# Expert tiles whose gathered rows are turned by VectorE after twelve moves per tile, and weights fetched by ScalarE's queue into two buffers

## What is computed

```python
x = x + tanh(g_xattn[0]) * ssm(ctx_1024, layernorm(x), ...)      # a selective scan (Mamba), 16 states, 512 channels
h = layernorm(x)
scores = softmax(h @ gate_w.T); the 6 best of 16 experts, weights normalised
out = sum over the chosen experts e of c[t, e] * swiglu_e(h[t])   # 512 -> 352 gate and up, 352 -> 512 down
out = out + swiglu_shared(h)                                     # 704 wide, done as two experts of 352
x = x + tanh(g_ffn[0]) * out
```

## Time and profile before

| | |
|---|---|
| median of 3 runs | 1429.51 us (1429.09 to 1432.42) |
| profiled execution, its own time | 1428.72 us |
| its span, first to last instruction | 1426.5 us |
| TensorE busy, instructions | 1342.8 us (94%), 8480 |
| VectorE, ScalarE, GpSimd busy | 785.2 (55%), 730.5 (51%), 948.6 (66%) us |
| granted TensorE clock, mean | 0.979 |
| routed tiles in the profile | from 692.97 to about 1408 us |

### The profile page before, as it was taken

One profiled execution on the slowest core, in us unless ns is written; L12 is line 12 of the kernel. 1 busy time (PEld: TensorE's weight loads), 2 busy tenths in 40 slices (PEclk: granted clock), 3 DMA queues, 4 the chain that ended last, 5 costly groups with the idle time before them and its releaser, 6 DMA issues.

```text
span 1426.5 us, 31834 instructions
## 1 busy us (share of the span) xinstructions
PE 1342.8 (94%) x8480; PEld 1208.7 (85%) x8481; DVE 785.2 (55%) x1364; ACT 730.5 (51%) x1317; POOL 948.6 (66%) x671
## 2 busy tenths in 40 slices
PE   6898998998898899999999999999999999999996
PEld 2676787887888799999999999999999998999995
DVE  6889898898999854653333333333333333333331
ACT  5899897898889464343332333323333333333321
POOL 0589899998998757887456665566645666646632
PEclk8899999998999999999999999999999999999998
DMA  4121123122241454645455535555445544455432
GB/s 138 38 75 31 54 68 102 66 93 69 76 160 68 135 123 103 146 81 141 84 144 143 132 62 146 140 144 142 105 94 139 143 134 101 102 146 133 76 67 36
DMA packets 65042, 149.13 MB, mean 105 GB/s; under 512 B 16976, under 2 KB 17616, under 8 KB 62656
## 3 DMA queue, kind: packets, MB, share of 16 engines
q0 software_dynamic: 31024, 62.10, 22.8%
q1 hardware_dynamic: 33392, 81.21, 17.3%
q10 hardware_dynamic: 560, 4.98, 0.9%
HBM read 101.50 MB, written 48.99 MB: 105 GB/s over the span
## 4 chain that ended last, share of the span: by engine, by line
PE 63%; DVE 3%; issue 2%; DVEq 1%; ACT 1%; POOL 1%; ACTq 0%; POOLq 0%
PE bank L1719 19%; PE bank L1699 18%; PE bank L1700 17%; PE bank L1687 3%; PE bank L1710 3%; DVE hs L1172 1%; PE bank L1604 1%; PE bank L1590 1%; PE bank L1602 1%; DVEq L1375 0%; POOL hc L949 0%; ACT ah L862 0%; DVE sc L1226 0%; PE bank L1665 0%; DVEq L1369 0%
## 5 line engine op out<-in xcount | busy, mean ns | idle before, releaser
L949 POOL TENSOR_TENSOR hc<-hs,crow 128x512 f32<-128x512 f32 x254 | 322.4, 1305 | 87.3 <-DVE hs L1172 81.5
L1699 PE MATMUL bank<-w,xh 128*128 (+1 forms) x1088 | 366.3, 338 | 6.2 <-DVE am L1393 2.9
L1700 PE MATMUL bank<-w,xh 128*128 (+1 forms) x1088 | 351.1, 323 | 0.0
L1015 POOL DMA_INDIRECT out_x<-ys,aid x104 | 169.8, 1633 | 271.3 <-issue 213.6
L1172 DVE TENSOR_TENSOR_SCAN hs<-dA,bank 128x512 f32<-128x512 f32 x256 | 295.6, 1208 | 46.2 <-PE bank L1604 28.8
L1719 PE MATMUL bank<-w,ah 128*128 (+1 forms) x816 | 264.8, 405 | 2.7 <-DVE al L1399 2.7
L1399 DVE TENSOR_TENSOR al<-bank,ah 128x384 fp32r<-128x384 f32 x136 | 75.9, 558 | 330.9 <-ACT ah L862 326.1
L1699 PEld LDWEIGHTS bank<-w,xh 128*128 128x128 f32 x1088 | 204.4, 188 | 26.0 <-issue 21.0
L1700 PEld LDWEIGHTS bank<-w,xh 128*128 128x128 f32 x1088 | 206.4, 190 | 4.1
L868 ACT COPY ys<-bank 128x512 f32<-128x512 f32 x136 | 79.8, 587 | 200.5 <-PE bank L1719 200.5
L1700 PE MATMUL bank<-w,xl 128*128 (+1 forms) x544 | 175.9, 323 | 0.0
(11 more groups left out here) (184 smaller groups left out, 2064.2 us busy)
## 6 DMA issues: line engine op xcount, KB each, us to landing
wraw<-in_wall SPq DMA_DIRECT2D x16, 2176.0 KB
crow<-c_rows SPq DMA_DIRECT2D x64, 256.0 KB, 3.3
xt<-token_rows_turned SPq DMA_DIRECT2D x32, 256.0 KB, 3.2
out_x<-ys POOLq DMA_DIRECT2D x32, 256.0 KB, 4.2
wraw<-in_wall ACTq DMA_DIRECT2D x2, 2176.0 KB
token_rows<-rowb SPq DMA_DIRECT2D x4, 1028.0 KB, 6.1
xrow<-in_x SPq DMA_DIRECT2D x4, 1024.0 KB, 7.5
out_x<-xrow SPq DMA_DIRECT2D x4, 1024.0 KB, 4.9
```

The source lines that it names most:

```text
L949: nc.gpsimd.tensor_tensor(hc[:, j, :], hs[:, j, :], crow[:, n % 4, :], ALU.mult).then_inc(hc_done, 1)
L1015: pool.indirect_dma_start(out_rows, bass.IndirectOffsetOnAxis(ap=aid[:, s:s + 1], axis=0), ys[:, s, :], None, bounds_check=TOKENS - 1, oob ...
L1699: nc.tensor.matmul(gate_bank[:, 0:I], xx, columns(w, off + ww + k * 2 * I, I), start=first, stop=last)
L1700: mm = nc.tensor.matmul(up_bank[:, 0:I], xx, columns(w, off + ww + k * 2 * I + I, I), start=first, stop=last)
```

## The change

1. `norm_chunk` writes the normalised rows with their features permuted: block (b, a) of 32 features goes to place (a, b). Weight rows of shared sets 0 and 1 and of the gate are loaded in that order (`fetch_turned`, five DMAs a set, four for the gate).
2. `turn_x` is removed. In its place, per routed tile: SyncE issues 12 DMAs (`move`), each of a block of 32 partitions x 128 columns from `xt` to `xs`, so that quarter g of the partitions goes to column block g; ScalarE copies the four blocks that stay on their own partitions (`keep`, ahead of `a_high`); VectorE transposes 32x32 blocks of `xs` into `xq` (`turn`, ahead of `a_low`). `x_high` and `x_low` read `xq` in place of the PSUM bank. `gather` waits for the moves and the copies of the tile that had its buffer.
3. SyncE's fetches of weights go. ScalarE issues the fetch of set e+1 behind its `split_high(e)`, into one of two buffers (`raws`, at offsets 0 and `FAR`).
4. GpSimd reads the table once per tile: row 3 of `meta` now holds the number of the set at its first tile, and 0 elsewhere.

```diff
+Q = 32
+G = P // Q
+MOVES = G * (G - 1)
+FAR = 33280
-               8: [("exp", 3)], TT - 3: [("fetch", 2)]}
+               8: [("exp", 3)], TT - 3: [("fetch", 2)], TT + 5: [("fetch", 3)]}
+        raws = alloc(span, "raws", [P, FAR + WCOLS])
+        xs = alloc(ctx, "xs", [P, 4, TC * P])
+        xq = alloc(ctx, "xq", [P, 2, H])
...
+        def quarters_in(eng, t, s, m, who):
+            apart(eng, moved[s], 16 * MOVES * ((t - NS) // 4 + 1) if isinstance(t, int) else 16 * MOVES * (m + 1), who)
+            apart(eng, kept, t + 1, who)
+        def fetch_turned(eng, e):
+            for b in range(G):
+                eng.dma_start(wraw[b * Q:(b + 1) * Q, 0:W2AT].rearrange("c (a i) -> c a i", a=G),
+                              wall[e, :, b * 2 * I:(b + 1) * 2 * I].rearrange("(a c) i -> c a i", c=Q)).then_inc(raw_in, 16)
+            eng.dma_start(wraw[:, W2AT:WCOLS], wall[e, :, W2AT:WCOLS]).then_inc(raw_in, 16)
...
 @block.sync
-            def fetch(e):
-                at_least(sp, wl_done, e)
-                sp.dma_start(wraw[:], wall[bass.ds(e, 1)].rearrange("a p c -> p (a c)")).then_inc(raw_in, 16)
+            def move(t, s, m):
+                rows_in(sp, t, s, m, "sp")
+                apart(sp, xt_turned, t - 3, "sp")
+                for a in range(G):
+                    for g in range(G):
+                        if g != a:
+                            sp.dma_start(xs[a * Q:(a + 1) * Q, s, g * P:(g + 1) * P],
+                                         xt[g * Q:(g + 1) * Q, s, a * P:(a + 1) * P]).then_inc(moved[s], 16)
-            with sp.Fori(3, NX) as e:
-                fetch(e)
             sp.wait_ge(meta_ready, 2)
+            groups = routed_groups(sp)
+            with sp.Fori(0, groups) as i:
+                for k in range(4):
+                    move(4 * i + NS + k, k, i)
...
 @block.scalar
-                nc.scalar.activation(rowb[:, t, 0:H], xrow[:, b % 2, t, :], ACT.Identity, ...
+                nc.scalar.activation(rowb[:, t, 0:H].rearrange("p (a b c) -> p b a c", a=G, c=Q),
+                                     xrow[:, b % 2, t, :].rearrange("p (b a c) -> p b a c", a=G, c=Q), ACT.Identity, ...
@@ split_high
-                nc.scalar.copy(columns(w, (e % 2) * 2 * WCOLS, mine), wraw[:, 0:mine]).then_inc(wh_done, 1)
+                nc.scalar.copy(columns(w, (e % 2) * 2 * WCOLS, mine), raws[:, bass.ds((e % 2) * FAR, mine)]).then_inc(wh_done, 1)
+                apart(act, wl_done, e, "act")
+                act.dma_start(raws[:, raw_at(e + 1)], wall[bass.ds((e + 1) % NX, 1)].rearrange("a p c -> p (a c)")).then_inc(raw_in, 16)
@@ x_high
-                    source = banks[4][:]
+                    source = xq[:, s, :]
+            def keep(t, s, m=None):
+                rows_in(act, t, s, m, "act")
+                act.wait_ge(xt_turned, t - 3)
+                for a in range(G):
+                    own = nc.scalar.copy(xs[a * Q:(a + 1) * Q, s, a * P:(a + 1) * P], xt[a * Q:(a + 1) * Q, s, a * P:(a + 1) * P])
+                own.then_inc(kept, 1)
@@ the loop
                     t, s = 4 * i + PEELED + k, (3 + k) % 2
+                    keep(t + 1, k, i)
                     a_high(t - 1, 1 - s)
...
 @block.gpsimd
@@ gather
-                    apart(pool, xt_turned, t - 3, "pool")
+                    quarters_in(pool, t - 4, s, m, "pool")
                     apart(pool, cc_done, t - 3, "pool")
-            def next_weights(t):
-                e = pool.value_load(meta[0:1, 2, bass.ds(t, 1)], min_val=0, max_val=NX - 1)
+            def starting_set(t):
+                return pool.value_load(meta[0:1, 3, bass.ds(t, 1)], min_val=0, max_val=NX)
+            def next_weights(number):
+                e = pool.snap(number % NX)
                 with pool.If(e > 0):
                     split_low(e)
-            def expert_starts(t, k):
-                first = pool.value_load(meta[0:1, 3, bass.ds(t, 1)], min_val=0, max_val=1)
-                with pool.If(first > 0):
+            def expert_starts(number, t, k):
+                with pool.If(number > 0):
                     all_added(t, k)
...
 @block.vector
+            def turn(t, s4, m=None):
+                quarters_in(dve, t, s4, m, "dve")
+                dve.wait_ge(xh_done, t - 1)
+                nc.vector.transpose(xq[:, s4 % 2, :].rearrange("p (b g r) -> p g b r", g=G, r=Q),
+                                    xs[:, s4, :].rearrange("p (g b c) -> p g b c", g=G, c=Q)).then_inc(xt_turned, 1)
@@ tile
                 s = s4 % 2
+                if not (isinstance(t, int) and t + 1 < NS):
+                    turn(t + 1, (s4 + 1) % 4, m)
                 a_low(t - 1, 1 - s)
...
 @block.tensor
-            def turn_x(t, s, m=None):
-                rows_in(pe, t, s, m, "pe")
-                at_least(pe, xl_done, t)
-                for k in range(HK):
-                    mm = nc.tensor.transpose(banks[4][:, k * P:(k + 1) * P], xt[:, s, k * P:(k + 1) * P], ident[:])
-                mm.then_inc(xt_turned, 1)
@@ tile
                 up(t, s, (2, 3), off)
-                if more and not (isinstance(t, int) and t + 1 < NS):
-                    turn_x(t + 1, (s4 + 1) % 4, m)
                 number = set_number(ahead) if ahead is not None else None
                 down(t - 1, 1 - s, old)
```

More of the change, by code:

```diff
@@ L356, in mamba_moe @@
         mem.close()
+        span = ExitStack()
+        raws = alloc(span, "raws", [P, FAR + WCOLS])
+        span.close()
         wraw = alloc(ctx, "wraw", [P, WCOLS])
@@ L447, in mamba_moe @@
         gathered = [sem(f"gathered{i}") for i in range(4)]
+        moved = [sem(f"moved{i}") for i in range(4)]
+        kept = sem("kept")
         zero_done = sem("zero_done")
@@ L595, in step @@
                     sp.wait_ge(summed, (b - 1) * DS * J + J * J)
-                    fetch(0)
+                    fetch_turned(sp, 0)
                 if b == NB - 1 and n == DS - 1:
@@ L986, in split_low, with gather @@
                 apart(pool, wh_done, 2 * (e + 1), "pool")
-                nc.gpsimd.tensor_tensor(columns(w, at + WCOLS, WCOLS), wraw[:], columns(w, at, WCOLS), ALU.subtract).then_inc(wl_done, 1)
-            def gather(t, s):
+                nc.gpsimd.tensor_tensor(columns(w, at + WCOLS, WCOLS), raws[:, raw_at(e)], columns(w, at, WCOLS), ALU.subtract).then_inc(wl_done, 1)
+            def gather(t, s, m=None):
                 if isinstance(t, int) and t < NS + 4:
@@ L1061, in _ @@
             pool.wait_ge(meta_ready, 2)
-            groups = routed_groups(pool)
-            with pool.Fori(0, groups - 2) as i:
+            looped = pool.value_load(fours[0:1, 2:3], min_val=E // 4 - 2, max_val=ROUTED // 4 - 2)
+            with pool.Fori(0, looped) as i:
                 for k in range(4):
                     t = 4 * i + NS + k
-                    gather(t + AHEAD, (k + AHEAD) % 4)
-                    next_weights(t)
-                    expert_starts(t, k)
+                    gather(t + AHEAD, (k + AHEAD) % 4, i + (k + AHEAD - 4) // 4)
+                    number = starting_set(t)
+                    next_weights(number)
+                    expert_starts(number, t, k)
                     add(t, k)
@@ L1072, in _ @@
                 if k + AHEAD < 8:
[L1073 to L1075 removed]
+                    gather(rest + k + AHEAD, (k + AHEAD) % 4, looped + (k + AHEAD - 4) // 4)
+                number = starting_set(rest + k)
+                next_weights(number)
+                expert_starts(number, rest + k, k % 4)
                 add(rest + k, k % 4)
@@ L1727, in offset_of, with tile @@
                 return pe.snap((number + 1) % 2 * (2 * WCOLS))
-            def tile(t, s4, old, off, more=True, m=None, ahead=None):
+            def tile(t, s4, old, off, ahead=None):
                 s = s4 % 2
@@ L1767, in _ @@
                     apart(pe, wl_done, number, "pe")
-                    number = tile(4 * i + PEELED + k, (3 + k) % 4, old, off, True, i, 4 * i + PEELED + k + 1 if k < 3 else None)
+                    number = tile(4 * i + PEELED + k, (3 + k) % 4, old, off, 4 * i + PEELED + k + 1 if k < 3 else None)
                     old = off
@@ L1773, in _ @@
             apart(pe, wl_done, number, "pe")
-            tile(last, 3, old, off, False)
+            tile(last, 3, old, off)
             turn_a(last, 1)
```

49 lines of the change are left out of this document (31 added, 18 removed).

## The result

The changed kernel took 1581.0 us (median of 4 runs, 1578.0 to 1590.5) against 1431.0 for the kernel before beside it: a ratio of 1.106 [1.100, 1.111]. The forecast was 1420 us with a range from 1394 to 1449; the change is 150 us slower than the kernel before, beyond every rival. The profiled execution has a span of 1576.0 us.

The account below looks back on a forecast made before the run. TensorE was taken to bound the routed tiles, busy 703.1 of 708.0 us. Terms -45.8 + 22.5 + 5 + 4.4 + 4.5 = -9.4 us on 1428.7, plus 0.8, gave 1420 us, range 1394 to 1449.

Parts of the forecast that it names:

- every rival: Three alternative outcomes for the whole kernel: 1401 us (chance 0.2), 1461 us (0.14) and 1432 us (0.24).
- the paragraph on `x_low`: Routed tiles: `x_low` with two SBUF inputs takes 1.080 us for 0.692, covered; GpSimd's split perhaps 2 x 0.39 us longer.
- items 6 and 7: First routed tile: 12 moves land late, +4.4 us once; every tile: SyncE needs 6.0 us beside 6.29, keeping pace.
- rival B: Routed tiles: SyncE's twelve issues a tile become the bound, 0.55 us each, 6.9 a tile; 1461 us, chance 0.14.
- Item 1: Routed tiles: `turn_x` leaves TensorE, 104 x 0.44 = -45.8 us, so a routed tile takes 6.29 us.
- item 3: Ordinary routed tiles: `turn` on VectorE takes 0.65 us ahead of `a_low`, which has slack; cost 0.
- Item 5: 26 loop starts: `a_low` has less in hand while TensorE's sequencer reads the table, 0.2 us each, +5 us.
- Item 2: ScalarE ahead of `a_high`: four `keep` copies of 0.296 us, overlapping by 0.10, end 0.88 us after the first starts.
- Item 4: 15 split tiles: `keep` and `turn` are uncovered and delay `down` by 1.5 us each, +22.5 us; bounds 13 and 53.
- Item 8: Rows after the 15 weight splits: gathered late, moved barely on time, 0.3 us each, +4.5 us; bounds 0 and 22.
- Item 9: At no cost: permuted write, extra DMAs for sets 0 and 1, second raw buffer, early fetches, fewer GpSimd table reads.

Follow-up runs that it names:

- e2: Kernel before, with `x_low` in routed tiles reading the gathered rows in SBUF instead of the turned ones in PSUM: 1580.5 us.
- e9: Changed kernel, with GpSimd's `split_low` a copy of the raw weights with one input: 1558 us.
- f12: Changed kernel, with `turn` writing PSUM and `keep` behind `gate_up` for the tile after next; all 12 moves on SyncE: 1558.1 us.
- e7: Changed kernel, with `turn` writing PSUM, eight moves a tile, and `keep` behind `gate_up` for the tile after next: 1431.7 us.
- e3: Changed kernel, with the bytes of a tile's 12 moves carried in 8: 1580.2 us.
- h1: g4 with VectorE's loop order changed: `x_low` right behind `a_low`, `multiply` ahead of the table read for the additions: 1418.2 us.
- e4: Changed kernel, with `turn` writing PSUM and eight moves a tile in place of 12: 1445.0 us.
- f4: e7 with four moves a tile in place of eight, each carrying three blocks side by side: 1420.7 us.
- g4: Changed kernel, with `turn` writing PSUM in steps of 4, four moves of 128 partitions a tile and no `keep`; all numbers computed: 1429.8 us.
- h2: Kernel before, with only the VectorE order of h1; its time is not given, the order alone gave nothing.
- e8: Kernel before, with only ScalarE's weight fetches into two buffers and GpSimd's one table read per tile: 1431.7 us.
- e1: Changed kernel, with `turn` writing a PSUM bank from which `x_low` and `x_high` read: 1560.6 us.
- e5: Changed kernel, with `split_low` in eight pieces of 544 columns; time not given, `x_low` still held at 14 of the 15 splits.

## Why the prediction was wrong, step by step

Two steps failed, and each alone was enough to put the time past the range: `x_low` at nothing, and 0.475 us for an issue of SyncE.

**The first is the paragraph on `x_low`**, outside the numbered sum: "`x_low` itself is covered", and GpSimd's split longer by 2 x 0.39 us. It read the `delta` sum's 1.080 us beside GpSimd's products as a shared rate, and applied it to the wrong side. That mean hides what one line's view of the kernel before shows:

```profile
L1150 DVE TENSOR_TENSOR delta<-delta,du x16: 683/1060/1760, 28.0 to 361.7; 128x512 f32<-128x512 f32 x16
```

Such a sum took 0.68 to 0.69 us with no GpSimd instruction beside it. The other 11 all ended 0.54 to 0.55 us after the GpSimd instruction that had begun before them, just as `x_low` does, and the GpSimd product that followed, at ten of them, took 1.72 to 1.75 us where its median is 1.28. It is a hold, first of one engine and then of the other, and no shared rate. Applied to a `split_low` of 9.6 us, this gives some 9 us and not 0.39, 15 times: 15 x 8.3 (9.0 less its own 0.69) = 125 us, less what slack there is. e2 measured 148, with the low clock behind the stands (0.70 to 0.80 over the tile). So the trace was not silent. GpSimd's `split_low` did not grow at all (9.41 for 9.60): it had begun first each time.

The Trainium skill has it outright, on a page that the prediction did not draw on: SBUF — State Buffer, section Who interferes with whom, says that a VectorE instruction with two SBUF inputs contends with a GpSimd instruction that reads SBUF, that this is an exclusive lock, and that the order of issue decides who blocks. The traces of e2 and e9 agree (`x_low` up to 9.5 us where it began later, and 2.93 beside a copy with one input), but for e2's one `x_low` that began first and was held all the same.

**The second is items 6 and 7, and with them rival B's price: 0.475 us between issues.** The forecast priced the moves by seven loads of another kind. Measured are 0.590 each and 0.63 apart: 7.6 us a tile for my 6.0, over the bound of 0.54 that the prediction had set for B. B's mechanism is real, and it cost 126 us between 8 and 12 moves (f12 less e7), where I had 104 x 0.09 + 22 = 31: B took the old stage's 6.81 us as what SyncE has to beat, and 12 x 0.63 is 0.8 over it. The first routed tile lost 5.8 us (12.95 for 7.19) for my 4.4, and the one behind it 1.5 more. What the pace costs beside the holds is another matter: 1 us (e3).

**Item 1, -45.8 us.** TensorE does issue a plain tile in 6.29; h1 reaches it in every tile inside a pass. But the mean of the 74 others fell by 0.11 to 0.14 only (changed kernel, e4, e7, f4), and by 0.02 in g4. Part of this was VectorE's row: inside a pass 6.60 in g4 and 6.29 in h1. The prediction took VectorE as a third busy and asked only for `a_low`'s slack; the chain in g4 goes through the table reads and `multiply`. The same order gives the kernel before nothing (h2), so the row came to bind with the turn on VectorE, and item 3's "cost 0" was wrong, by about 0.3 a plain tile in g4; that it is `turn` itself was not tried alone.

**Item 5** had 0.35 + 0.2 = 0.55 us for a loop start over a plain tile. The changed kernel has that (7.08 for 6.52), but g4 has 0.76, e4 0.85 and h1 1.1 (7.40 for 6.29). In h1 TensorE stands there for `multiply`; why VectorE is late just there no run shows.

**Item 2** was right in kind: the copies are 0.296 each, but do not overlap (four take 1.21 us, in the timeline of ScalarE), where I had 0.88:

```profile
1193.04 1.21 ACT L909 COPY xs<-xt 32x128 f32<-32x128 f32 x4
```

**Item 3's** price of `turn`, 0.65, is 0.71. **Item 4** (whose turn ends at 1016.12 and not at 1016.15, which changes nothing) made the split tile 6.87 - 0.44 + 1.5 = 7.9; with hold and pace gone it was 8.38 (e4), and e7's early copies took 1.46 of it away. **Item 8**, late rows: with eight moves the tiles behind splits are no later than before (7.24 for 7.23); with nine they lose 1.0 us, so it depends on SyncE's room, as B had it. **Item 9** was right: e8 for the fetches, the buffers and the table read, and for the permuted write and the extra DMAs ahead of it the start of the first routed stretch (685.68 us, before 685.78). ScalarE's fetch is issued inside the weight copy (1191.53 for 0.36, inside 1191.13 to 1193.15), at no cost.

Two errors hid behind each other: without the hold the time would have been 1561 (e1), without the pace 1580 (e3), both past the range; without either it is 1445 (e4), inside it.

## What to carry to other kernels

Before an operand moves from PSUM to SBUF, count the SBUF inputs of each VectorE instruction that reads it, and look for the longest GpSimd instruction, or row of them, that it can start beside: that length is the price. Eight pieces in a row did not lower it at 14 splits of 15; a PSUM operand did at all. Price DMA issues by the queue's time for that kind of transfer times their number against the shortest tile, and make few wide ones: four issues did what twelve and four copies had done (g4). When two causes can each fill the same time, undo both together too: alone they gave 20 and 1 us here, together 136.

## What the runs showed of the hardware that I had not expected

- The hold ends 0.54 to 0.57 us after GpSimd's last instruction, whether that was 9.4, 3.8 or eight of 1.3 us in a row (but for one split of e5); its own length hardly matters.
- Two SBUF inputs are not the only case. In the kernel before, a `tensor_scalar` of VectorE with one SBUF input and its output in SBUF took 0.42 us alone and up to 1.53 beside GpSimd, and where it had begun after a GpSimd instruction it ended 0.28 us after that one's end:

```profile
L1144 DVE TENSOR_SCALAR st<-sw x16: 420/881/1533, 26.1 to 335.8; 128x512 f32<-128x512 f32 x16
```

- An SBUF-to-SBUF move between 32-partition quarters took SyncE 0.59 us at the median, whether it carried one block (f12) or two; 0.584 with three (f4), and 0.597 with four in 128 partitions (g4).
- VectorE's transpose of 128x512 takes 0.71 us into SBUF, 0.726 into PSUM, also with a step of 4 elements in its output, and is not held by GpSimd.
- After a stand of some 8 us the granted clock over a tile was 0.70 (part of it at 1.2 GHz: a product each 0.29 us for 0.16): 9.11 us of products for 6.5.
